# Scores of four small attentions on 32-row TensorE tiles, two heads to a tile

## What is computed

```python
def small_attention(q, k, v, mask_and_scale):       # q: 64 x 256, k, v: 64 keys (layer 2: 64 + 64) x 256
    q, k, v = (split(a, heads=16, head_dim=16) for a in (q, k, v))
    scores = einsum('hqd,hkd->hqk', q, k)           # contraction over 16 features only
    probs = softmax(mask_and_scale(scores), axis=-1)
    return einsum('hqk,hkd->hqd', probs, v)

x = L0(x, ctx)                                      # 8 heads of 64, 256 x 256 scores
x = x + tanh(gate) * small_attention(x, layernorm(ctx)) @ Wo                            # stage b
x = mlp(rmsnorm(small_attention(x, concat(ctx, x)) @ Wo + x)) + x                       # stage e, two key blocks
x = x + small_attention(layernorm(x), layernorm(x), mask=self) @ Wao                    # stage c
x = x + small_attention(layernorm(x), ctx, mask=cross) @ Wco; x = x + mlp(layernorm(x)) # stage f
```

## Time and profile before

| | |
|---|---|
| median of the three timed runs | 1386.85 us |
| the profiled execution, its own time | 1382.49 us |
| its span, first to last instruction | 1380.5 us |
| TensorE matmul busy | 1287.4 us, 93% |
| VectorE busy | 1049.5 us, 76% |
| ScalarE busy | 808.0 us, 59% |
| GpSimd busy | 770.8 us, 56% |
| score matmuls of the small attentions (L689) busy | 88.5 us |

### The profile page before, as it was taken

The page is one execution under the profiler, slowest core; times in us unless marked ns, Lnnn a source line. Parts: engine busy times, 40 slices in busy tenths (PEclk is TensorE's granted clock), DMA queues, the critical chain, the costliest instruction groups (busy, mean ns, idle before and its releaser), DMA issues. The chain is left out here.

```text
span 1380.5 us, 34075 instructions
## 1 busy us (share of the span) xinstructions
PE 1287.4 (93%) x12668; PEld 975.6 (71%) x12668; DVE 1049.5 (76%) x2226; ACT 808.0 (59%) x2101; POOL 770.8 (56%) x1056
## 2 busy tenths in 40 slices
PE   6999999999999989999899999999999999979675
PEld 5767668686877868677686867768676776857464
DVE  4788896868789696977968787796969878685642
ACT  4657575565657565565666657565655746554332
POOL 2564575556657474665665557565655656563431
PEclk9999999999999999999999999999999999999896
DMA  8100000000000000000000000000000000000000
GB/s 315 37 3 17 2 19 9 17 11 5 18 6 17 11 17 11 6 17 7 17 7 22 6 10 17 8 17 11 16 11 2 21 7 2 7 1 6 1 4 5
DMA packets 23584, 25.72 MB, mean 19 GB/s; under 512 B 10624, under 2 KB 22912, under 8 KB 23168
## 3 DMA queue, kind: packets, MB, share of 16 engines
q1 hardware_dynamic: 23424, 23.55, 5.4%
HBM read 21.44 MB, written 2.10 MB: 17 GB/s over the span
## 5 line engine op out<-in xcount | busy, mean ns | idle before, releaser
L588 POOL TENSOR_SCALAR p_a<-p_a,rec_a 128x256 f32<-128x256 f32 x512 | 245.8, 497 | 99.1 <-DVE rec_a L543 98.8
L574 ACT ACTIVATE p_a<-bank,nmax_a 128x256 f32<-128x256 f32 x512 | 236.8, 476 | 91.3 <-DVE nmax_a L536 90.7
L536 DVE TENSOR_REDUCE nmax_a<-bank 128x2 f32<-128x512 f32 x256 | 166.9, 680 | 13.5 <-PE bank L486 13.2
L601 PE MATMUL bank<-ident,p_a 128*128 128x128 f32 x1024 | 144.7, 277 | 6.0 <-POOL p_a L588 2.7
L486 PE MATMUL bank<-k_a,q_a 64*128 64x256 f32 x1024 | 138.7, 396 | 2.9 <-ACT p_a L574 1.1
L617 PE MATMUL attended<-p_a,v_a 128*64 128x256 f32 x1024 | 133.9, 389 | 4.2 <-DVE p_a L635 1.6
L601 PEld LDWEIGHTS bank<-ident,p_a 128*128 128x128 f32 x1024 | 113.7, 141 | 33.6 <-issue 25.2
L486 PEld LDWEIGHTS bank<-k_a,q_a 64*128 64x128 f32 x1024 | 91.7, 186 | 32.9 <-issue 22.6
L574 ACT ACTIVATION_READ_ACCUMULATOR p_a<-bank,nmax_a 128x1 f32 x512 | 105.8, 207 | 0.0
L617 PEld LDWEIGHTS attended<-p_a,v_a 128*64 128x64 f32 x1024 | 65.4, 136 | 54.5 <-issue 27.9
L635 DVE COPY p_a<-bank 128x512 f32<-128x512 f32 x128 | 86.1, 679 | 14.7 <-PE bank L601 14.3
(11 more groups left out here) (235 smaller groups left out, 3098.7 us busy)
## 6 DMA issues: line engine op xcount, KB each, us to landing
wb<-in_wb SPq DMA_DIRECT2D x1, 4096.0 KB, 12.6
wc<-in_wc SPq DMA_DIRECT2D x1, 4096.0 KB, 24.3
xc<-in_x SPq DMA_DIRECT2D x16, 128.0 KB, 2.7
xc<-in_ctx SPq DMA_DIRECT2D x16, 128.0 KB, 2.9
c_top<-in_ctx SPq DMA_DIRECT2D x16, 128.0 KB, 2.8
res_a<-in_x SPq DMA_DIRECT2D x16, 128.0 KB, 2.1
k_c<-in_ctx SPq DMA_DIRECT2D x16, 128.0 KB, 2.1
out<-y_out SPq DMA_DIRECT2D x16, 128.0 KB, 1.7
```

What stands on the lines that cost most here:

```text
L536: dve.tensor_reduce(nmax_a[:, n, e, :], ps[:, :].rearrange("p (q k) -> p q k", q=KT), AX.X, ALU.max, negate=True).then_inc(A.s["max"], 1)
L574: last = act.activation(p_a[:, j % 2, n, e, qt, :], ps[:, qt * D:(qt + 1) * D], ACT.Exp, bias=nmax_a[:, n, e, qt:qt + 1], accum_out=sum_a[ ...
L588: last = pool.tensor_scalar(p_a[:, j % 2, n, e, qt, :], p_a[:, j % 2, n, e, qt, :], rec_a[:, n, e, qt:qt + 1], 1.0, ALU.mult, ALU.mult)
L601: last = nc.tensor.transpose(ps[:, kt * D + qt * P:kt * D + (qt + 1) * P], p_a[:, j % 2, n, e, qt, kt * P:(kt + 1) * P], ident[:, :])
```

## The change

The array is used as eight 32 x 64 tiles instead of four 64 x 64 tiles. A group of 32 rows (`g`, four of them) holds two heads. `kblk` therefore keeps only two spread copies (`HQ` = 2) for each half and sequence instead of four, and one GpSimd instruction makes it for both halves. A key block takes four banks, each filled in its first 256 columns only; sixteen matmuls (`f` x `b` x `g`) have 32 x 64 weights and 32 x 128 of moving data. VectorE reads four banks of 128 x 256 for each key block. The order of heads in `T.p` changes with it, and the product with the values picks them accordingly; its shapes stay. A mask `half_mask` is made at the start, and the scratch `rows` moves from `E.kblk` to `E.p`, so that the wait for the end of its use (`ready`) moves from the first GpSimd spread of stage e to VectorE ahead of the first masked read of stage e. `ORDER` is written anew for all engines (TensorE's has the same 1492 steps, VectorE's grows from 1606 to 1766, GpSimd's falls from 786 to 706), and `BANK` grows from 1637 to 1797 fills.

```diff
+QUADS = 4
+QR = P // QUADS
+HQ = QR // HD
-    return (tuple((("s", c, 0), ("s", c, 1)) for c in range(blocks))
+    return (tuple(tuple(("s", c, g) for g in range(QUADS)) for c in range(blocks))
...
-            T.kblk = t("kblk", [P, KT, blocks, 2, HR, S])
+            T.kblk = t("kblk", [P, blocks, KT * 2, HQ, S])
...
-        rows, = views(E.kblk[:, :, :, :, :, :].rearrange("p f c b h k -> p (f c b h k)"), ((P, len(ROWS), D),))
-        spread, = views(E.p[:, :, :].rearrange("p f k -> p (f k)"), ((P, 3 * KT, P),))
+        spread, rows = views(E.p[:, :, :].rearrange("p f k -> p (f k)"), ((P, 3 * KT, P), (P, len(ROWS), D)))
...
-                pe.wait_ge(T.s[kblk], T.at(i, kblk, KT))
-                bs = [fill_bank(T, pe, i, ("s", c, r)) for r in range(KT)]
+                pe.wait_ge(T.s[kblk], T.at(i, kblk, 1))
+                bs = [fill_bank(T, pe, i, ("s", c, g)) for g in range(QUADS)]
                 for f in range(KT):
                     for b in range(2):
-                        for r in range(KT):
-                            rows_ = slice(r * S, (r + 1) * S)
-                            last = mm(bs[r][b * S:(b + 1) * S, f * D:(f + 1) * D], T.qT[rows_, f, b * S:(b + 1) * S],
-                                      T.kblk[rows_, f, c, b, :, :], start=True, stop=True)
+                        for g in range(QUADS):
+                            rows_ = slice(g * QR, (g + 1) * QR)
+                            last = mm(bs[g][b * S:(b + 1) * S, f * P:(f + 1) * P], T.qT[rows_, f, b * S:(b + 1) * S],
+                                      T.kblk[rows_, c, 2 * f + b, :, :], start=True, stop=True)
                             if f == KT - 1 and b == 1:
-                                filled(T, last, i, ("s", c, r))
+                                filled(T, last, i, ("s", c, g))
...
-                            for g in range(HR // 2):
+                            for g in range(QUADS // KT):
                                 n = 2 * r + g
                                 last = mm(ps[32 * n:32 * (n + 1), f * P + b * S:f * P + (b + 1) * S], T.v[:, c, b, 4 * f + n, :, :],
-                                          T.pt[:, r, c, 2 * f + g, b * S:(b + 1) * S], start=c == 0, stop=c == blocks - 1)
+                                          T.pt[:, r, c, 2 * g + f, b * S:(b + 1) * S], start=c == 0, stop=c == blocks - 1)
...
             for c in range(blocks):
-                for r in range(KT):
+                for g in range(QUADS):
                     yield
-                    ps = wait_fill(T, dve, i, ("s", c, r))
-                    ins = masked(c, ps[:, :].rearrange("p (h k) -> p h k", h=HB), heads_of(T, r)[:, c, :, :])
-                    release(T, ins, i, ("s", c, r))
+                    ps = wait_fill(T, dve, i, ("s", c, g))
+                    heads = heads_of(T, g // 2)[:, c, g % 2 * (HB // 2):(g % 2 + 1) * (HB // 2), :]
+                    release(T, masked(c, ps[:, 0:D].rearrange("p (h k) -> p h k", h=HB // 2), heads), i, ("s", c, g))
...
-            for f in range(KT):
-                yield
-                if i == 0:
-                    if T is E:
-                        ready(pool, i)
-                    pool.wait_ge(setup["consts"], ROW_MASK)
-                else:
-                    for r in range(KT):
-                        wait_fill(T, pool, i - 1, ("s", c, r))
-                written(V, pool, i, name)
-                keys = T.kT[:, c, f, :].rearrange("p (b k) -> p b k", b=2)
-                pool.tensor_tensor(T.kblk[:, f, c, :, :, :], bc(keys, 2, HR), bc(bc(row_mask[:, :], 2, S), 1, 2), ALU.mult).then_inc(T.s[kblk], 1)
+            yield
+            if i == 0:
+                pool.wait_ge(setup["consts"], ROW_MASK)
+            else:
+                for g in range(QUADS):
+                    wait_fill(T, pool, i - 1, ("s", c, g))
+            written(V, pool, i, name)
+            keys = T.kT[:, c, :, :].rearrange("p f (b k) -> p (f b) k", b=2)
+            pool.tensor_tensor(T.kblk[:, c, :, :, :], bc(keys, 2, HQ), bc(bc(row_mask[:, :], 2, S), 1, 2 * KT), ALU.mult).then_inc(T.s[kblk], 1)
```

More of the change, by code:

```diff
@@ L139 @@
[L139 to L147 removed]
+        "nnsknnaakaaaaddaddadddadaddddksnakkdnkddkssaakdkkddaaaddddadddannabddbdknbddnddaaadbbdbddbakddkaeddeededeadded"
@@ new lines @@
+        "adcanbnbaeedadaaeddedednfedaandfeddeddfedaedddedffaafdkkfkddkckfcbcfcfkbkbkbcfbfaaeddeeceeacedcacddnnbdbaeeaee"
+        "dfdaefddfeaddaddedeeffdefaafkkedkddfdkckkbkfkcccbbfbcbfefeeeededddddcdcccdeebeebfefefeeeeffefkkkfckkkbkckcfcfb"
+        "bfbcbfefeeeececcceeeefefefeeefefefkfccccfcffcfcfccffffffffffff"),
+    "act": (
+        "knnaakaaaadasadaaadaadaaaakadkdaaakkkaadadaaadaannbadbadbabdbbaabaaakdaeadaeaddaeaaneandababeeadaeeaaeabbkbbad"
+        "bdeaeeaadaceadaacacecddaccaaceneaadnaabadbaaaeedaadeeafeadaadeaafafadeffefkkkdcfkkbbcfbbfbccaeacaaeccbabennedd"
+        "aaeeaadafaaeedaaedfedafaeffeaafakkkckfcbbfbbfkbeccedccacdeeaanaaaneebdadabaaeeafeaaddeaafedefaadaffaaacfkkkkck"
+        "fbbfbbfdcbcdeaacaaecacednnebdbaeefaaeadaeaeadaadeaafdfeeffaaaafkkkcaakfcbbkfbbfbdccedcaaeaccenneddbebeaeeaaaef"
+        "aaeaddaaeeffdcfaafacfaakkkakfcdcffkbbccbcbbaaeadaeadfdnenedaabeebaaaeeaaedadadeaafefdeafafaafdckkkkkbbcdfbabfb"
+        "faeccecaacceanendbabadaaaeedaadeefaeadaaedaaaeeaffdfafadfackkkackfkabbbbfbfccdeaaebdnnbcececeaeaaeefaeaddaefaf"
+        "eeaaffdafckkakkfkcbbfbbfbccdecceacaedadaeaabdanbneedaeeaeaadfaeaaedeffaadffaafckkkaakkfbbcbfbfabccdeaeccddecea"
+        "aanbeabeadnadaeeaaaefdaeadaaefedffaadfafaakckkkkfbcbfbbfdcbcadeaacececnedaabanbedeaaeaaefdaedaaeaafedefaafdfac"
+        "fakkkkfbcbkffbbccbaeedcadceceanbanabaedeaaedaeaaeafdaaedaaedeffdaaffaafakkkdckfbcbfbfkbbccaedaacecaacaednebnbe"
+        "aeaeedfaaaedadfeafeffeaafaakkaadkdfckkbbcbbfbfecceddcececeebeebfeeffeefffkkkckkbbfcbbfbfecceccceeeeeefeeffeeff"
+        "fkccfccffcccfffffffff"),
@@ L203 @@
 NORM = {"stats": 1, "mv": 1, "eps": 1, "rstd": 1, "xn": 1}
-SOFTMAX = {"kblk": KT, "max": KT, "sub": KT, "exp": KT, "sum": KT, "rec": KT, "prob": KT}
+SOFTMAX = {"kblk": 1, "max": KT, "sub": KT, "exp": KT, "sum": KT, "rec": KT, "prob": KT}
 RAISED_K = {"c_in": 16, **NORM}
 RAISED_B = {"m_in": 32, "mask": 1, **SOFTMAX}
-RAISED_E = {"m_in": 32, "mask": 1, "res": 2, "kblk_own": KT, **SOFTMAX, **NORM, "msq": 1, "hid": 2}
+RAISED_E = {"m_in": 32, "mask": 1, "res": 2, "kblk_own": 1, **SOFTMAX, **NORM, "msq": 1, "hid": 2}
 RAISED_C = {"res": 1, "madd": KT, **SOFTMAX, **NORM}
@@ L247, in build @@
         head_mask = sb("head_mask", [P, HB])
-        row_mask = sb("row_mask", [P, HR])
+        half_mask = sb("half_mask", [P, HB // 2])
+        row_mask = sb("row_mask", [P, HQ])
         cols = sb("cols", [P, NCOLS])
@@ L725, in pe_attention, with quads_of @@
             filled(T, last, i, "p")
+        def quads_of(r):
+            return range(2 * r, 2 * r + 2)
         def heads_of(T, r):
@@ L744, in dve_attention @@
                     for c in range(blocks):
-                        written(T, dve, i, ("s", c, r))
+                        for g in quads_of(r):
+                            written(T, dve, i, ("s", c, g))
                 v = heads_of(T, r)
@@ L803, in pool_attention @@
                     mask_ready(pool)
-                    written(T, pool, i, ("s", 0, r))
+                    for g in quads_of(r):
+                        written(T, pool, i, ("s", 0, g))
                     v = heads_of(T, r)[:, 0, :, :]
@@ L1060, in dve_e @@
             dve.wait_ge(E.s["mask"], E.at(i, "mask", 1))
+            ready(dve, i)
             def masked(c, ps, dst):
                 if c == 0:
-                    return dve.scalar_tensor_tensor(dst, ps, 1.0 / HD, bc(m2[:, :], 1, HB), ALU.mult, ALU.add)
+                    return dve.scalar_tensor_tensor(dst, ps, 1.0 / HD, bc(m2[:, :], 1, HB // 2), ALU.mult, ALU.add)
                 return dve.tensor_scalar(dst, ps, 1.0 / HD, None, ALU.mult)
```

122 lines of the change are left out of this document (57 added, 65 removed).

## The result

The changed kernel takes 1368.5 us (median of four runs, 1367.11 to 1369.8) beside 1386.64 us for the kernel before: a ratio of 0.987, 95% interval 0.9853 to 0.9887, or 18 us. The forecast was 1359 us, 28 us less than before. The profiled execution took 1367.11 us, 15.4 us less than the profiled one of before.

The account below looks back on a forecast made before the run. TensorE was taken to set the pace. From the profiled 1382.5 us, 31.0 and 1.7 off and 5 added gave 1354.8, or 1359 us for the median; own range 1351 to 1369, wider range 1345 to 1386.

Parts of the forecast that it names:

- shorter score steps: TensorE's score step falls from 1.03 to 0.60 us: 31.0 us over 72 middle steps, 1.7 us over the other eight.
- masked reads: On VectorE, four smaller reads cost 0.14 us more per key block, 11 us in all, none of it on TensorE.
- relief of GpSimd: Some 85 us less spreading on GpSimd, counted as 0, with a bound of a few us of gain in the tail.
- banks, order, what is left: TensorE's idle time in the middle grows as VectorE's slack shrinks: 5 us more; the rewritten order counted as nothing.
- Rival 2: At TensorE's score step, eight tiles don't run side by side; it stays at 1.03 us, kernel about 1390 us; chance 0.06.
- what shortens one of its steps shortens the kernel nearly one for one: TensorE sets the pace in the long middle, with only 28.6 us of 1000 idle, so its savings count almost fully.
- instruction fetching: Possible cause of 5.9 us unexplained TensorE idle time ahead of the score step; could double, 6 us at most.
- rival 1: Score step starves on banks, TensorE waiting for VectorE's third and fourth read: slower, up to 1413 us; chance 0.12.
- The sequence of TensorE's steps has the same length, and I count nothing for it: All five engine queues are rewritten; the new order was counted as 0 us, either way.
- The sign by which I meant to know a bad order: TensorE's middle share at 94% or less with the score step at 0.60 us: the order, not the tiles, decided.
- rival 3: Half the gain: score step costs some 0.8 us or banks take back half; 1371 to 1383 us by median; chance 0.20.

Follow-up runs that it names:

- the searched order: The changed kernel with only its order and bank strings replaced, found by a second, longer search against a model of traced durations: 1332.51 us, ratio 0.9608.
- the table of four combinations: Old and new tiles, reads and spread, each in old and new segment order: old tiles 1387 and 1422 us, new tiles 1376 and 1368.5 us.

## Why the prediction was right and wrong

The sign, the range and the mechanism of the step hold. The sum was 10 us too good: what a shorter step is worth was put at twice its size, and two terms put at 0 were not 0 and partly made up for it, which is luck. The change in us, as forecast and as the runs have it:

| term | forecast | measured | from |
|---|---|---|---|
| shorter score steps | -32.7 | -15.7 (-18.0 in the searched order) | four tiles against eight |
| masked reads | 0 | about +3 | reads in halves |
| relief of GpSimd | 0 | -11.3 | half the spread |
| banks, order, what is left | +5 | about +6 | by subtraction |
| sum | -27.7 | -18.1 | the two kernels |

The terms come from different orders and needn't add up; the last one is only what the others leave, and no run measured it alone. One run measured the last three together: -2 us, by the changed kernel with four tiles against the kernel before, where the forecast had +5.

The two profiled executions give the same miss in another way. The forecast has TensorE 32.7 us less busy and 5 us more idle, 27.7 us in all. Measured are 25.7 us less busy and 10.6 us more idle, 15.1 us. About half of the 12.6 us that are missing is busy time. With four tiles TensorE is busy for 1291.8 us in the changed kernel and for 1287.4 in the kernel before, so other parts of the change added 4.4 us that the prediction counted at nothing.

**The score step.** Its price was right: 0.62 us where I took 0.60, by the rounds of the earlier trace rows and the matmuls of the earlier trace rows. Rival 2 (tiles not side by side) is refuted by the change itself, and the kernel with four tiles shows the 1.03 us that it would have had. Behind that stands the Trainium skill, TensorEngine Tiling (Array Packing), section Instruction Overhead: an estimate from its 60 or so cycles for each matmul would have made the step 0.80 us. 32 matmuls in 0.62 us are 19 ns each, so the trace disagrees for matmuls on eight different tiles.

**What a saved microsecond is worth.** This is the step that failed: "what shortens one of its steps shortens the kernel nearly one for one", concluded from 971 busy us of 1000 and from no wait over 3 us. TensorE was busy for 97%, and still about half of the steps' 32 us was lost, in two orders (15.7 and 18.0 us arrived). Most of what is missing is to be seen in the trace as waits (12.5 and 9.8 us), and the largest of these lie where no step was changed: at transposes that wait for VectorE's and GpSimd's results. A reading of why: the 28.6 idle us of the middle were already the places at which TensorE came earlier than its operands, and a TensorE that comes there 0.4 us earlier waits 0.4 us more. This reading fits two other runs, in which TensorE's work wasn't touched at all: 67 us less of GpSimd gave 11 us, 9 us more of VectorE cost about 3 (1 to 5). If TensorE alone bounded the kernel, neither would have shown. That it is these chains, step by step, is argued; that the pace is shared is shown.

**GpSimd's relief.** Counted at 0 with "a bound of a few us of gain", it is 11.3 us, the second largest term. The profile had the hint: 5.9 us ahead of the score step with no releaser, for which I named only instruction fetching. It was mostly the wait for keys: it fell to 1.2 us with half the spread. I had called the 1.0 us by which keys come earlier worth nothing because the list of waits named no GpSimd keys there; the row without a name was the place.

**Masked reads.** 0.13 us more a key block was forecast as 0.14, and by the run with the reads in halves it isn't free either.

**Banks and order.** 5 us is close to the 6 that are left over, but a remainder can't show that it was right, and the reason wasn't mine. In the old order the changed kernel pays 14.8 us of bank waits at the score step (rival 1 at a quarter of its price), and in the new one 3.5 us in the same two groups. "The sequence of TensorE's steps has the same length, and I count nothing for it": the table of four combinations shows 7 us one way and 35 the other. The sign by which I meant to know a bad order (TensorE's share in the middle at 94% or less) was not there: the share is 96%.

**The case that came true** lies between two. By the profiled execution, which took 1367 us, it is rival 3, half of it (1366 and up). By the median, 1368.5, it is 2.5 us under rival 3's range and just inside the forecast's own, 1351 to 1369. And rival 3's two reasons (a step of 0.8 us, or banks that take back half) are both refuted: the step is 0.62 us, and banks cost 3.5 us. What took back most of it was waits behind the step, on operands.

**Two banks in place of four** would have kept the reads whole. It wasn't tried, since two row tiles that run at once would write the same bank. The same page of the Trainium skill, section Gotcha 1: PSUM Pressure, says that different row tiles can't access one bank at the same time; no run here shows it.

## What to carry to other kernels

A busy share of 97% on one engine doesn't say that a microsecond saved on it is a microsecond gained: with queues in a fixed order and other engines at 50 to 80%, it was about half here, in two orders. Count the relief of the other engines too. Idle time ahead of a step for which the trace names no releaser can be a wait for another engine, as it was here; find out before calling it free. After a change of durations, fit the order again for both versions before comparing them: it was worth 36 us here for the changed kernel, twice the change itself, and 27 us for the one before.

## What the runs showed of the hardware

Eight 32 x 64 tiles run side by side: 32 matmuls with 128 moving columns take 0.62 us, the same 32 on four 64 x 64 tiles 1.03 us. A round of products on 32 rows takes as long as one on 64 rows (0.11 us for 128 columns in both); only more tiles at once shortened the step.

A load of a function table on ScalarE takes 1.283 us each time. Runs had 52 to 74 of them, and the fastest of all had 74.

The same matmuls took 18.1 us less of TensorE's busy time in an order with 149 fewer changes of tile shape, and 14.9 us less with 134 fewer: 0.11 to 0.12 us a change, if it is these. Other pairs of runs give 0.04 and 0.21 us.
